# Channel mix: where the values, the sigmoid and the norm's mean stand in a round; and the last round of the time mix

## The chip, the cores and the metric

One core of a Trainium2 chip runs the whole program in one launch. The time is the device time in microseconds (us) of that core. Each of its engines has a queue of its own that it works through in order: TensorE (PE: matrix products, weight loads beside them), VectorE (DVE), ScalarE (ACT), GpSimd (POOL) and SyncE (SP), which here only issues DMAs. Engines wait for each other through semaphores.

## The reference, cut to what matters

Four layers follow each other on S = 4096 tokens of D = 256 channels: an attention with two memories, a mixture of experts, a time mix with channel mix, and a ternary feed-forward layer. The change lies in the third:

```python
# time mix, its last steps (y, new_state from the WKV recurrence)
r = sigmoid(r * tmr + x_prev * (1.0 - tmr))
x = x + r * y
# channel mix
xp = concatenate([x[:, -1:], x[:, :-1]], axis=1)
xn = _layernorm(x, g2, b2)
kk = (xn @ W_cm) * cmk4 + xp4 * (1.0 - cmk4)          # 1024 keys
rr = sigmoid(xn * cmr + xp * (1.0 - cmr))
vv = square(relu(kk)) @ W_cp
x = x + rr * vv
```

The block of tokens 0 needs the last token of the sequence as its previous one, so it is computed last.

## The kernel before, in words

Tokens are handled in NB = 8 blocks of BT = 512, channels on the partitions (256 channels = KT = 2 planes of 128; 1024 keys = KH = 8 planes, worked in PAIRS = 4 pairs). Each product of fp32 numbers is three products of high and low halves (L1468 to L1470), so every operand is split: ScalarE writes the rounded high half, VectorE subtracts it for the low half. The order on each engine is written out by hand, engine by engine, inside a program block; a new block starts when all engines have left the one before.

**The time mix block** (L1849 to L2338). In round `b` VectorE runs the recurrence (`sums`, `differences`, `exponents`, `values`, `result`), ScalarE the exponentials and, in `shares`, the sigmoid (L2170, another table than exponential and logarithm, so a table load). `result(b)` ends with xa (L2015), which GpSimd adds by DMA to `after_time_mix` in memory (L1897); when that add has landed (`xa_out`), GpSimd adds the block of `after_time_mix` to `residual_sum` (L1900). In the last round the norm of the channel mix's first block (tokens 1) is worked in between: mean, centred, squares, variance, `first_scaled` (L2035), `first_normed` (L2185, writes XN and its high half XN0h), `first_low_part` (L2039, the low half XN0l), `first_key_part`, and TensorE's `first_keys` (L2315: 16 of the first 24 products of keys, those that need only XN0h). `second_centred` (L2031) takes the mean off the second block.

**The channel mix block** (L2369 to L2770), rounds `b` = 0 to 7, with `place(b)` the block of tokens.
- TensorE, in round `b`, for each pair `i`: `up(b, i)` (12 products of keys), `down(b-1, i)` (12 products of values of the round before, into banks 6 and 7), and in between `mean(b+1)` behind `up(b, 0)` and `variance(b+1)` behind `down(b-1, 1)`. `up(b, 0)` waits for the low half of the normed input; `down(b-1, 0)` waits until the values before are taken from banks 6 and 7 (`ev_d`). In round 0, `up(0, 0)` and `up(0, 1)` are only the eight products with XN0l (L2712).
- VectorE: `keys` (L2527, reads a bank), `square_keys` (L2533), `low` (L2537, low half of the squares), `receptance` (L2517), `centre` (L2503), `scale` (L2507), `low_x` (L2511), `values` (L2544, reads banks 6 and 7), `residual` (L2551).
- ScalarE: `high` (L2643, high half of the squares), `squares` of the centred input (L2618), `deviation` (table load L2622, Ln L2624, Exp L2626), `parts` (L2611, L2613), `normed` (L2633, L2637), `sigmoid` of the receptance (table load and L2647), and `low_halves` (L2656: a check of the next layer's weights, twice a round).
- GpSimd: `sum_mean` (L2482) and `sum_squares` (L2487) add the two planes of the input and of its squares, so that one product with a matrix of 1/256 gives mean and variance.
- SP, in order: `load(b+3)` (the input and its shift by one token; waits until the place has been read by `normed` and `parts`), `store(b)` (waits for `residual(b)`), `load_sum(b+2)` (waits for the store), then a weight of the next layer in rounds 0 and 1, and a block of 1 MB of hidden weights (L2442).

Of the kernel before, what the change touches and what calls it, by code (L numbers as in the profile page):

```python
# [19 lines left out]
KT = D // 128  # L20
# [56 lines left out]
def build(nc, A):  # L77
# [5 lines left out]
    with ctx:  # L83
# [1806 lines left out]
        def _(pool):  # L1890
# [3 lines left out]
            def add_to_sum(b):  # L1894
# [4 lines left out]
                pool.wait_ge(xa_out, 16 * (b + 1))  # L1899
                pool.dma_start(byk(sx_d)[:, :, b * BT:(b + 1) * BT], byk(xa_d)[:, :, b * BT:(b + 1) * BT],  # L1900
                               accum_op=ALU.add).then_inc(sx_out, 16)
# [9 lines left out]
        def _(dve):  # L1911
# [91 lines left out]
            def result(b):  # L2003
# [4 lines left out]
                go(V.tensor_tensor(YA, prev(AV), V_, ALU.subtract))  # L2008
                dve.wait_ge(sg_d, b + 1)
# [62 lines left out]
            first_low_part()  # L2072
# [3 lines left out]
        def _(act):  # L2076
# [122 lines left out]

            A_.activation(wtm[0][:, :, :], wst, ACT.Copy).then_inc(wth_rdy, 1)  # L2200
# [17 lines left out]
            for b in range(NB):  # L2218
# [15 lines left out]
                weights(b)  # L2234
                if b + 1 < NB:
                    taken(b + 1, 1)
                    exps(b + 1)
# [3 lines left out]
                if b + 1 < NB:  # L2241
                    gates(b + 1)
                else:
                    first_normed()
                    first_key_part()
                if b + 2 < NB:
                    inner(b + 2)

        @block.tensor
        def _(pe):  # L2250
# [64 lines left out]
            def first_keys():  # L2315
# [48 lines left out]
        hm, hv = rs, in_x_tok(1536, BT)  # L2364
# [36 lines left out]
        def _(sp):  # L2401
# [43 lines left out]
            sp.wait_ge(hw_add, 16 * 16)  # L2445
            for j in range(3):
# [28 lines left out]
        def _(pool):  # L2475
            P = nc.gpsimd

            def sum_mean(b):
                pool.wait_ge(cin_ld[b % 2], loaded(b))
                pool.wait_ge(xs_rdy, b)  # L2480
# [8 lines left out]
            for b in range(1, NB + 2):  # L2489
                if b >= 2:  # L2490
                    sum_mean(b)
# [3 lines left out]
        def _(dve):  # L2495
# [57 lines left out]
            for b in range(NB):  # L2553
                nxt = b + 1 < NB
                if b >= 2:
                    values(b - 2)
# [8 lines left out]
                if b == 0:  # L2565
                    receptance(0)
                else:
                    centre(b + 1)
                for i in range(1, PAIRS):
                    keys(b, i)  # L2570
                    if b >= 1 and i == PAIRS - 1 and nxt:
# [4 lines left out]
                    if b == 0 and i == PAIRS - 2:  # L2576
                        low_x(1)
                    low(b, i - 1)
                    if b == 0 and i == 1:
                        scale(1)  # L2580
                if nxt:
                    receptance(b + 1)
            values(NB - 2)
# [854 lines left out]
```

## Time and profile before

| what | us |
|---|---|
| median of 3 runs (2006.26 to 2007.89) | 2007.76 |
| the profiled execution | 2017.27 |
| its span, first to last instruction | 2015.1 |
| channel mix: first keys to the first gates of the next layer | 1202.42 to 1419.40 |

Over the span PE is busy 91%, DVE 74%, ACT 55%, POOL 15%; the mean granted clock of TensorE is 0.955. A row of the timeline reads: start, duration, engine, line, operation, what is written from what, count; and in brackets how long the engine had been idle before, and what ended it.

### The profile page before, as it was taken

What the parts mean: (1) busy time and instruction counts of PE and PEld (TensorE: products, weight loads), DVE (VectorE), ACT (ScalarE), POOL (GpSimd) and SP (SyncE); (2) the same over time, 40 slices, a digit from 0 to 9 for tenths busy, and PEclk for the clock granted to TensorE, in tenths of its full rate; (3) what the DMA queues carried; (4) which work ended last, traced back from release to release, by engine and by line L of the source; (5) the groups of instructions that cost most, each with busy time, mean ns of one, the idle gap of its engine ahead of it and who ended that gap; (6) DMA issues with size and microseconds to landing.
All of it is one profiled execution on the core that took longest, in us unless ns stands there. A gap on an engine that the chain in (4) does not pass through costs nothing. (4 is left out here: it accounts for less than half of the span.)

```text
span 2015.1 us, 31198 instructions
## 1 busy us (share of the span) xinstructions
PE 1829.8 (91%) x10840; PEld 1563.2 (78%) x10840; DVE 1489.5 (74%) x2966; ACT 1114.9 (55%) x1987; POOL 307.6 (15%) x282
## 2 busy tenths in 40 slices
PE   8999999996499999999677758999999999999999
PEld 5688888885499999999455536677788888888887
DVE  7567888886477666766599889998676776776675
ACT  4656666653344443443688857665456456456454
POOL 0001012233333323333100011111000000000000
PEclk9999999996699999999788889999999999999999
DMA  3199434413346545344434553333333143143141
GB/s 110 50 382 404 137 119 142 145 65 107 120 97 135 114 89 115 63 74 69 126 105 91 108 106 136 148 124 123 124 138 146 36 175 145 42 176 117 53 177 64
DMA packets 107986, 251.79 MB, mean 125 GB/s; under 512 B 8992, under 2 KB 51616, under 8 KB 99616
## 3 DMA queue, kind: packets, MB, share of 16 engines
q1 hardware_dynamic: 82288, 201.16, 28.3%
q0 software_dynamic: 23680, 46.28, 12.6%
q10 hardware_dynamic: 1888, 2.67, 0.4%
q8 instruction: 75, 1.23, 0.3%
q14 instruction: 55, 0.45, 0.1%
HBM read 172.88 MB, written 107.61 MB: 139 GB/s over the span
## 5 line engine op out<-in xcount | busy, mean ns | idle before, releaser
L1542 POOL DMA_INDIRECT tokens_behind_spare_rows<-yg,row_of_token x70 | 119.2, 1702 | 298.7 <-DVE row_of_token L1733 277.0
L1666 ACT ACTIVATE h<-bank,b1s 128x256 f32<-128x256 f32 x280 | 123.7, 472 | 36.3 <-PE bank L1470 21.1
L3175 ACT ACTIVATE hidden_quarter<-hidden_quarter,scl 128x512 f32<-128x512 f32 x96 | 67.6, 721 | 118.9 <-DVE hidden_quarter L3011 118.9
L1655 ACT ACTIVATE yg<-yt,own_gates 128x256 f32<-128x256 f32 x68 | 30.9, 502 | 184.0 <-DVE yt L1728 177.2
L1223 PE MATMUL bank<-st,L 128*128 128x128 f32 x768 | 117.2, 279 | 13.3 <-DVE st L573 13.2
L957 ACT ACTIVATE L<-bank 128x512 f32<-128x512 f32 x128 | 74.5, 594 | 95.7 <-PE bank L1215 84.7
L2384 PE MATMUL bank<-split_0h,hidden_weights 128*128 128x512 f32 x320 | 126.5, 395 | 0.0
L2384 PE MATMUL bank<-split_1h,hidden_weights 128*128 128x512 f32 x320 | 125.4, 392 | 0.1
L2385 PE MATMUL bank<-split_0l,hidden_weights 128*128 128x512 f32 x320 | 125.3, 391 | 0.0
L2385 PE MATMUL bank<-split_1l,hidden_weights 128*128 128x512 f32 x320 | 125.3, 391 | 0.0
L1215 PE MATMUL bank<-L 128*128 128x128 f32 x640 | 119.1, 276 | 1.2 <-ACT L L957 1.2
L573 DVE TENSOR_TENSOR st<-st,bank 128x256 f32<-128x256 f32 x192 | 75.3, 417 | 54.0 <-PE bank L1223 53.0
L1223 PEld LDWEIGHTS bank<-st,L 128*128 128x128 f32 x768 | 100.5, 193 | 17.8 <-DVE st L573 7.0
L1214 PE MATMUL bank<-L 128*128 128x128 f32 x512 | 100.9, 279 | 0.7
L2384 PE MATMUL bank<-split_2h,hidden_weights 128*128 128x512 f32 x256 | 101.4, 396 | 0.0
L1762 DVE TENSOR_TENSOR hsl<-h,hsh 128x512 fp32r<-128x512 f32 x140 | 96.9, 692 | 4.8
L2385 PE MATMUL bank<-split_2l,hidden_weights 128*128 128x512 f32 x256 | 100.2, 391 | 0.0
L1215 PEld LDWEIGHTS bank<-L 128*128 128x128 f32 x640 | 95.1, 193 | 1.4 <-ACT L L957 1.4
L2963 DVE SCALAR_TENSOR_TENSOR hidden_quarter<-bank,scl,x_tok 128x512 f32<-128x512 f32 x64 | 47.5, 749 | 56.2 <-ACT x_tok L3138 56.2
L1468 PE MATMUL bank<-xTh,w_1h 128*128 128x256 f32 x288 | 81.7, 284 | 7.2 <-ACT h L1666 7.2
L1468 PE MATMUL bank<-xTh,w_0h 128*128 128x256 f32 x272 | 77.7, 286 | 9.8 <-DVE xTl L1720 5.2
L2970 DVE TENSOR_TENSOR split_2l<-hidden_quarter,split_2h 128x1024 fp32r<-128x1024 f32 x48 | 59.2, 1254 | 35.4 <-ACT split_2h L3157 35.4
(485 smaller groups left out, 6028.1 us busy)
## 6 DMA issues: line engine op xcount, KB each, us to landing
hidden_weights<-hidden_weight_blocks SPq DMA_DIRECT2D x64, 1024.0 KB, 4.8
z_by_expert<-zero SPq DMA_DIRECT2D x64, 520.0 KB, 15.7
hidden_weight_blocks<-in_ffn_dram SPq DMA_DIRECT2D x14, 1024.0 KB
ckb<-in_ffn_dram POOLq DMA_DIRECT2D x32, 352.0 KB, 5.0
xg<-z_by_expert SPq DMA_DIRECT2D x36, 260.0 KB
x_tok<-in_w_dram SPq DMA_DIRECT2D x8, 1024.0 KB
x_tok<-x_T SPq DMA_DIRECT2D x16, 512.0 KB, 6.1
x_tok<-after_time_mix SPq DMA_DIRECT2D x15, 512.0 KB, 8.4
```

Source lines behind the costliest of these rows:

```text
L573: V.tensor_tensor(z_ if SQUARES <= n < LEVELS - 1 else x_, x_, B[2 + j][:, 0:256], ALU.subtract if n == 0 else ALU.add).then_inc(ap_rdy, 1)
L957: A_.activation(L[:, p, j, (n + 1) % 2, :, :], src, ACT.Copy).then_inc(sq_cp, 1)
L1214: T.matmul(B[j][:, 256 * m:256 * m + 128], b_, a, start=True, stop=True)
L1215: last = T.matmul(B[j][:, 256 * m + 128:256 * m + 256], a, b_, start=True, stop=True)
L1223: last = T.matmul(B[2 + j][:, 0:256].rearrange("p (a m d) -> p a m d", a=2, m=2)[:, :, m, :], Ln[:, 2 * m + 1, :], right, start=True, stop ...
L1468: nc.tensor.matmul(out, a[0], b[0], start=first, stop=False)
L1542: pool.indirect_dma_start(x2_d, bass.IndirectOffsetOnAxis(to_row[:, j:j + 1].bitcast(u32), 0), yg[:, j, :], None, compute_op=ALU.add).then ...
L1666: nc.scalar.activation(h32[:, m, :], B[m % 4][:, 0:TT], ACT.Gelu_apprx_tanh, bias=b1s[:, e * KH + m:e * KH + m + 1]).then_inc(h_act, 1)
L1762: V.tensor_tensor(hs[1][:, m:m + 2, :], h32[:, m:m + 2, :], f32(hs[0][:, m:m + 2, :]), ALU.subtract).then_inc(h_rdy, 1)
L2384: nc.tensor.matmul(out, w, x[0], start=first, stop=False, **more)
L2385: return nc.tensor.matmul(out, w, x[1], start=False, stop=last, **more)
L3175: A_.activation(QB[to][:, m, :], src, ACT.Gelu, scale=scl[:, off[lay.name] + row:off[lay.name] + row + 1]).then_inc(g_act, 1)
```

## The change

In the time mix block: GpSimd leaves out the last round's add to `residual_sum` and its wait; VectorE takes `first_low_part` inside the last `result`, ahead of its wait for the shares; ScalarE takes `first_normed` ahead of the last `shares`, and then also loads the table of logarithms and squares the second block; TensorE takes the eight products with XN0l.

In the channel mix block: each engine's list is in another order. VectorE takes `values(b-1)` at the end of round `b`, behind the last squared keys, instead of at the start of round `b+1`; `receptance(b)` in round `b` instead of at the end of round `b-1`; `centre` ahead of the first square; `residual` behind `receptance`. ScalarE takes `sigmoid(b)` behind `squares(b+1)`. TensorE takes `mean(b+2)` at the end of round `b`. GpSimd's mean sum has a buffer of its own (`mean_halves`, before it shared `rs` with the deviation) and doesn't wait for `scale`. GpSimd issues the last add to `residual_sum` here; SP waits for the last add to `after_time_mix` ahead of the first hidden blocks.

```diff
@@ GpSimd, time mix @@
+                if b + 1 < NB:
                     pool.wait_ge(xa_out, 16 * (b + 1))
                     pool.dma_start(byk(sx_d)[...], byk(xa_d)[...], accum_op=ALU.add).then_inc(sx_out, 16)
@@ VectorE, time mix, result(b) @@
                 go(V.tensor_tensor(YA, prev(AV), V_, ALU.subtract))
+                if b == NB - 1:
+                    first_low_part()
                 dve.wait_ge(sg_d, b + 1)
@@ ScalarE, time mix @@
+            def second_squares():
+                act.wait_ge(xc_rdy, 2)
+                A_.activation(sq, IN[:, 1, 0, :, :], ACT.Square).then_inc(sqr_rdy, 1)
                 weights(b)
+                if b == NB - 1:
+                    first_normed()
...
-                    first_normed()
                     first_key_part()
+                    nc.scalar.preload_act_table_set(LOG_EXP)
+                    second_squares()
@@ TensorE, time mix, first_keys() @@
+                pe.wait_ge(xn_rdy, 1)
+                for m in range(4):
+                    for k in range(KT):
+                        last = T.matmul(B[2 + m][:, :], wcm[0][:, k, m * 128:(m + 1) * 128], XN0[1][:, k, :], start=False, stop=k == KT - 1)
+                    last.then_inc(cm_ps, 1)
@@ SP, channel mix @@
             sp.wait_ge(hw_add, 16 * 16)
+            sp.wait_ge(xa_out, 16 * NB)
@@ GpSimd, channel mix @@
                 pool.wait_ge(cin_ld[b % 2], loaded(b))
-                pool.wait_ge(xs_rdy, b)
                 pool.wait_ge(mean_ps, b)
...
-            for b in range(1, NB + 2):
-                if b >= 2:
-                    sum_mean(b)
+            sum_squares(1)
+            pool.wait_ge(xa_out, 16 * NB)
+            pool.dma_start(byk(sx_d)[:, :, S - BT:S], byk(xa_d)[:, :, S - BT:S], accum_op=ALU.add).then_inc(sx_out, 16)
+            for b in range(2, NB + 2):
+                sum_mean(b)
                 sum_squares(b)
@@ VectorE, channel mix @@
-                if b >= 2:
-                    values(b - 2)
                 if b >= 1:
                     low(b - 1, PAIRS - 1)
                 keys(b, 0)
+                if b >= 1:
+                    centre(b + 1)
                 square_keys(b, 0)
+                receptance(b)
+                if b == 0:
+                    scale(1)
                 if b >= 2:
                     residual(b - 2)
...
                     square_keys(b, i)
+                    if b >= 1 and i == PAIRS - 1:
+                        values(b - 1)
                     low(b, i - 1)
...
-                if nxt:
-                    receptance(b + 1)
@@ ScalarE, channel mix @@
             parts(0)
-            squares(1)
+            deviation(1)
             high(0, 0)
-            deviation(1)
+            normed(1)
             parts(1)
             high(0, 1)
-            normed(1)
             high(0, 2)
             sigmoid(0)
             high(0, 3)
-            sigmoid(1)
...
                 squares(b + 1)
+                sigmoid(b)
                 low_halves(b, 0)
...
-                if nxt:
-                    sigmoid(b + 1)
@@ TensorE, channel mix @@
             def mean(b):
                 pe.wait_ge(hm_rdy, b - 1)
+                pe.wait_ge(xc_rdy, b)
...
-                    if i == 0 and 1 <= b < NB:
-                        mean(b + 1)
                     if b >= 1:
                         down(b - 1, i)
-                    if i == 1 and b < NB:
+                    if i == 3 and b < NB:
+                        mean(b + 2)
+                    if i == (1 if b else 0) and b < NB:
                         variance(b + 1)
```

## Rows read from the trace of the kernel before

**Rows 1.** Busy time by round: stretch; length, then engines' busy us (instructions), granted clock, DMA share, GB/s
```profile
1202.42:1224.09 21.67, 16.11 (x53) 11.64 (x53) 21.06 (x23) 15.86 (x20) 2.54 (x2) 0.80 0.90 313
1224.09:1248.33 24.24, 23.23 (x99) 18.06 (x98) 22.84 (x25) 19.50 (x26) 3.45 (x2) 1.00 0.00 1
1248.33:1274.77 26.44, 24.28 (x102) 18.55 (x101) 24.22 (x25) 17.23 (x21) 3.57 (x2) 1.00 0.42 160
1274.77:1301.18 26.41, 24.26 (x102) 18.54 (x101) 24.19 (x25) 17.23 (x21) 2.60 (x2) 1.00 0.41 159
1301.18:1326.51 25.33, 24.27 (x102) 18.53 (x101) 23.11 (x25) 17.23 (x21) 2.58 (x2) 1.00 0.34 125
1377.18:1402.40 25.22, 23.50 (x100) 18.25 (x99) 23.92 (x25) 11.95 (x14) 3.44 (x2) 1.00 0.17 63
```
**Rows 2.** Timeline of the time mix's end and the next block's start
```profile
1185.23 1.28 ACT L2170 ACT_TABLE_LOAD   x1
1186.52 1.33 ACT L2170 ACTIVATE wkv_tmp<-wkv_tmp,uw 128x512 f32<-128x512 f32 x2
...
1189.30 1.06 ACT L2192 ACTIVATE XN0h<-XN 128x1024 fp32r<-128x1024 f32 x1
...
1190.50 0.77 PE L2323 MATMUL bank<-XN0h,wcmh 128*128 128x512 f32 x1 [14.72 <-ACT XN0h L2192]
...
1193.99 1.22 DVE L2041 TENSOR_TENSOR XN0l<-XN,XN0h 128x1024 fp32r<-128x1024 f32 x1
...
1194.59 1.22 POOL L1897 DMA_DIRECT2D after_time_mix<-wkv_tmp  x1 [9.88 <-DVE wkv_tmp L2015]
...
1195.12 1.21 DVE L2033 TENSOR_TENSOR x_tok<-x_tok,bank 128x1024 f32<-128x1024 f32 x1
...
1195.65 0.40 PE L2323 MATMUL bank<-XN0h,wcml 128*128 128x512 f32 x1
1200.90 1.15 POOL L1900 DMA_DIRECT2D residual_sum<-after_time_mix  x1 [5.09 <-POOLq L2338]
...
1201.10 1.33 ACT L2613 ACTIVATE rr<-x_tok,vec 128x512 f32<-128x512 f32 x2 [9.51 <-PEq L2338]
...
1202.42 1.53 DVE L2527 SCALAR_TENSOR_TENSOR kq<-bank,vec,kx 128x512 f32<-128x512 f32 x2 [6.09 <-PE bank L2712]
```
**Rows 3.** VectorE's timeline in round 4, whose first keys start at 1301.18
```profile
1303.76 1.22 DVE L2551 TENSOR_TENSOR x_tok<-rr,x_tok 128x1024 f32<-128x1024 f32 x1
...
1307.47 2.19 DVE L2533 SCALAR_TENSOR_TENSOR kq<-kq 128x1024 f32<-128x1024 f32 x1
...
1313.45 1.23 DVE L2507 TENSOR_TENSOR x_tok<-x_tok 128x1024 f32<-128x1024 f32 x1 [0.17 <-ACT x_tok L2626]
...
1319.45 1.23 DVE L2511 TENSOR_TENSOR XN1l<-XN,XN1h 128x1024 fp32r<-128x1024 f32 x1 [0.72 <-ACT XN1h L2637]
...
1322.86 1.41 DVE L2517 SCALAR_TENSOR_TENSOR rr<-XN,vec,rr 128x512 f32<-128x512 f32 x2
```
**Rows 4.** ScalarE's timeline in round 4
```profile
1306.14 1.06 ACT L2618 ACTIVATE x_tok<-x_tok 128x1024 f32<-128x1024 f32 x1 [1.21 <-DVE x_tok L2503]
1307.11 1.04 ACT L2656 ACTIVATE low_halves<-hidden_weights 128x1024 bf16<-128x1024 uint16 x1
...
1309.69 1.06 ACT L2643 ACTIVATE khh<-kq 128x1024 fp32r<-128x1024 f32 x1 [1.45 <-DVE kq L2533]
...
1324.30 1.06 ACT L2647 ACTIVATE rr<-rr 128x1024 f32<-128x1024 f32 x1
```
**Rows 5.** SP's store and load in round 2, and GpSimd's sum
```profile
1252.16 0.36 SPq L2430 DMA_DIRECT2D x_T<-x_tok  x1
...
1256.93 0.55 SPq L2418 DMA_DIRECT2D x_tok<-after_time_mix  x1
...
1266.69 2.28 POOL L2482 TENSOR_TENSOR x_tok<-x_tok 128x512 f32<-128x512 f32 x1 [10.96 <-DMA x_tok<-after_time_mix]
```
**Rows 6.** TensorE's timeline at the turn to round 5
```profile
1325.61 0.47 PE L1468 MATMUL bank<-khh,wcph 128*128 128x512 f32 x1 [0.99 <-DVE rr L2544]
```

More of the change, by code:

```diff
@@ L1898, in add_to_sum @@
                 pool.wait_ge(x2_out[b % 2], 16 * (b // 2 + 1))
-                pool.wait_ge(xa_out, 16 * (b + 1))
-                pool.dma_start(byk(sx_d)[:, :, b * BT:(b + 1) * BT], byk(xa_d)[:, :, b * BT:(b + 1) * BT],
-                               accum_op=ALU.add).then_inc(sx_out, 16)
+                if b + 1 < NB:
+                    pool.wait_ge(xa_out, 16 * (b + 1))
+                    pool.dma_start(byk(sx_d)[:, :, b * BT:(b + 1) * BT], byk(xa_d)[:, :, b * BT:(b + 1) * BT],
+                                   accum_op=ALU.add).then_inc(sx_out, 16)
             for done in second_sems:
@@ L2071, in _ @@
                 result(b)
-            first_low_part()
             second_centred()
@@ L2363, in build @@
         low_out = sb("low_halves", [128, 1024], mybir.dt.bfloat16, to=pd)
-        hm, hv = rs, in_x_tok(1536, BT)
+        hm, hv = sb("mean_halves", [128, BT], to=pd), in_x_tok(1536, BT)
         hm_rdy, hv_rdy = sem("mean_halves_summed"), sem("square_halves_summed")
@@ L2553, in _ @@
             for b in range(NB):
-                nxt = b + 1 < NB
-                if b >= 2:
-                    values(b - 2)
                 if b >= 1:
@@ L2561, in _ @@
                 keys(b, 0)
+                if b >= 1:
+                    centre(b + 1)
                 square_keys(b, 0)
+                receptance(b)
+                if b == 0:
+                    scale(1)
                 if b >= 2:
                     residual(b - 2)
[L2565 to L2568, printed above, removed]
                 for i in range(1, PAIRS):
                     keys(b, i)
-                    if b >= 1 and i == PAIRS - 1 and nxt:
+                    if b == 0 and i == 2:
+                        low_x(1)
+                    if b >= 1 and i == PAIRS - 1 and b + 1 < NB:
                         low_x(b + 1)
@@ L2575, in _ @@
                     square_keys(b, i)
-                    if b == 0 and i == PAIRS - 2:
-                        low_x(1)
+                    if b >= 1 and i == PAIRS - 1:
+                        values(b - 1)
                     low(b, i - 1)
-                    if b == 0 and i == 1:
-                        scale(1)
-                if nxt:
-                    receptance(b + 1)
-            values(NB - 2)
             low(NB - 1, PAIRS - 1)
@@ L2620, in deviation @@
             def deviation(b):
-                if b <= NB:
+                if 1 < b <= NB:
                     nc.scalar.preload_act_table_set(LOG_EXP)
@@ L2709, in up @@
                 if b == 0 and i < 2:
-                    for m in (2 * i, 2 * i + 1):
-                        for k in range(KT):
-                            last = nc.tensor.matmul(B[2 + m][:, :], wcm[0][:, k, m * 128:(m + 1) * 128], XN0[1][:, k, :],
-                                                    start=False, stop=k == KT - 1)
-                        last.then_inc(cm_ps, 1)
                     return
@@ L2737, in _ @@
                         up(b, i)
-                    if i == 0 and 1 <= b < NB:
-                        mean(b + 1)
                     if b >= 1:
                         down(b - 1, i)
-                    if i == 1 and b < NB:
+                    if i == 3 and b < NB:
+                        mean(b + 2)
+                    if i == (1 if b else 0) and b < NB:
                         variance(b + 1)
-                    if i == 3 and b == NB - 1:
-                        mean(NB + 1)
                     if i == 1 and b == NB:
```

## The prediction

> **What bounds the kernel now.** I read the page first: TensorE is busy 91% of the span, and the chain that ended last is almost only the last layer's products (L2384, L2385). That chain begins at 1419.4 us, when the channel mix block has ended, and it is dense from there. So whatever the channel mix ends earlier goes through to the end one for one, and the time mix tail is worth what it lets the channel mix start earlier. Next I cut the channel mix into its rounds at each first key instruction [rows 1]. Round 0 takes 21.67 us, the rounds behind it 24.24 to 26.44. In round 4 VectorE is busy 23.11 of 25.33 us, TensorE 24.27 (this counts overlapped ends; started every 0.23 us, 96 products take 21.9 and the two means 2.1, together 24.0) and ScalarE 17.2. No engine is full: a chain through all of them sets the round. The timeline of round 4 shows it [rows 3, 4]. Squared keys 1 end at 1309.66, their high half starts on ScalarE at 1309.69, then come table load, Ln and Exp, and `scale` at 1313.45: 3.76 us behind. `low_x` follows 6.00 us after `scale` (square, high half, norm, its high half). From `low_x` to the next round's first key VectorE has 7.06 us of dense work (1319.45 to 1326.51). Keys that wait for TensorE lie ahead of `scale` and cost nothing. TensorE itself stops about 1 us a round for the values' instruction (L2544) [rows 6]; that is slack, not the bound.
>
> The seam between the blocks is the other place [rows 2]. VectorE is through at 1196.33, but nobody starts before 1201.1: GpSimd must first see its last add to `after_time_mix` land (issued 1194.59, seen 1200.90, so 6.3 us) before it may issue L1900 and leave. Then VectorE waits until 1202.42 for the low products (L2712).
>
> **The seam, part by part.** ScalarE: `first_normed` (1187.76 to 1190.36, about 2.6 us) goes ahead of the table load at 1185.23. Its input is scaled by 1184.3, so it ends near 1187.8. The shares (1.28 for the table and 1.33) end 2.6 us later than before, near 1190.4. VectorE has, since L2008 at 1189.07, moved `first_low_part` (1.22) to exactly there: it runs 1190.2 to 1191.4 and covers the later shares. The same five instructions follow L2008 as before in another order, so `second_centred` still starts at 1195.12 and ends 1196.33; the last xa is 1.13 later, and with it the add: issued 1195.7, landed near 1202.0. TensorE's 16 products start at 1187.8 instead of 1190.50; they took 5.5 us to 1196.0, the eight low ones 3.5 in the next block, so all end by 1196.8 at the latest. ScalarE now also squares block 1: 1196.35 to 1197.4. GpSimd no longer waits for the add to land. So the last to leave is ScalarE at 1197.4 and the next block starts at 1197.6: 3.5 us earlier. If GpSimd's issue (1195.7 plus 1.22) must end first, nothing changes.
>
> In the new block the keys' products are there already, so the first key starts at 1197.6, not at 1202.42: 4.8 us. What was behind the removed wait: GpSimd now does the squares' half sum, then waits until 1202 for the add and issues its DMA, and its first mean sum needs the load that SP issued before, which is not in by then. SP gets one more wait (1202) ahead of the three hidden blocks. Behind it is `load(3)`, which waits for `parts(1)` near 1208 anyway, and ScalarE wants the first hidden block only at 1215. Bounds for this wait: 0, and 3 us if the blocks land late; I take 0.
>
> **Round 0.** VectorE's list: 4 keys (1.44 each), 4 squares (1.14), 4 low halves (1.13), receptance 1.32, scale 1.14, low_x 1.14: 18.5 us. Receptance 1 (1.32) has gone to round 1 and the waits with it. ScalarE stays ahead of each: Exp ends near 1201.5 and `scale` comes at 1201.6; normed and its high half are ready at 1205.5 for a `low_x` at 1207.9. One collision may stay. When GpSimd adds while VectorE works from SBUF alone, VectorE's instruction takes 1.0 us more (2.19 against 1.23 in the row at 1307.47 [rows 3]); keys read PSUM and are not held up (1316.95 to 1318.2 in round 4). I take half of it, 0.6. Round 1 starts at 1216.7 instead of 1224.09: **-7.4 us**, 1.3 of which are only handed on.
>
> `mean(2)` now stands in TensorE's queue ahead of `up(1,0)`. Its load is issued by 1201.3 and lands between 5 and 9.8 us later [rows 5], its sum and mean take 2.3: 1208.6 to 1213.4. `up(1,0)` needs 2.7 us, or 5.1 at the 1.2 GHz level, which the rows show behind idle stretches (products every 0.43 us instead of 0.23). So it is there at 1211.3 to 1218.5, around 1216.7. I take 0; the bad end is +1.8.
>
> **A later round.** Offsets from the first key. VectorE: key 0, centre 1.37, square 2.51, receptance 3.65, residual 4.97, key 6.10, square 7.54. ScalarE: high half 3.77, squares 4.74 (4.96 before), and then what is new here: table load and sigmoid (1.28 and 1.06), 5.82 to 8.1, then the low halves (1.04 and 0.19), so high half 1 starts at 9.28. Before it was 1309.69 - 1301.18 = 8.51 [rows 1, 4]: **+0.77**. It was bound by the square, itself held 1.05 by GpSimd; that sum now falls at 6.2 to 7.4, under the PSUM keys, but this no longer helps, as ScalarE is late. From there 3.76 and 6.00 us as before, since all their members stay. Behind `low_x`: square, values, low, low; receptance is gone, **-1.32**. The moved `values` wait for the last down product (offset 19.4; they come at 21.3), and TensorE needs them only behind `up(b+1,0)` at 23.1, so its 1 us stop goes, for nothing. Sum: 25.33 + 0.77 - 1.32 = 24.8 us.
>
> The price of the moved load is its row: 1.28 us at 1185.23, and the next instruction 0.01 us behind it at 1186.52 [rows 2]. The Trainium skill ("ScalarE: Activation LUTs", section "What ACT_TABLE_LOAD costs") adds a drain of about 1380 ns to each load's 1283 ns; this trace doesn't show the drain, and by it the round would be an estimated 26.2 us.
>
> **The mean a round ahead.** In PE's queue it was behind `up(b,0)` of its own round; now it is ahead of `up(b+1,0)`, 2.7 us sooner, while its data come later: the load follows the store of residual(b-2), whose end moves from offset 3.8 to 6.2. From store to GpSimd's sum took 14.5 us in round 2 (1252.16 to 1266.69 [rows 5]); by the same timeline 14.4, 11.9, 13.1 and 10.4 in rounds 3 to 6. So the sum starts at 20.8, 20.6, 18.2, 19.4, 16.7. In round 2 it runs 21.4 to 22.6, the mean to 23.65, both first products to 26.5, and the second half of the next key, due at 25.5, ends 1.1 late. Behind such a delay TensorE runs late through the next round and holds `scale` by 0.35. Round 4 loses 0.3 and round 5 loses 1.1 to the sum's collision with `low_x` or a square. Rounds 2 to 6: 25.9, 26.25, 25.45, 25.9, 24.8 = 128.3, against 26.44 + 26.41 + 25.33 + 25.34 + 25.33 = 128.85: **-0.55**. Bounds: 124.0 if nothing of this bites, 133 if each is late by one more us.
>
> Round 1 goes from 24.24 to 24.8: **+0.55**. Round 7 gets receptance 7 but loses the collision (its mean sum falls at 16.5 to 17.7, under keys): `centre(9)` at 22.96 against 22.95. From there squares, half sum and variance lead to the same end: **0**; +0.8 if the collision stays.
>
> **Sum.** -7.4 + 0.55 - 0.55 + 0 = -7.4 us. The profiled execution took 2017.27 us (span 2015.1 and 2.2 around it) and would take 2009.9; it lies 9.5 above the median of 2007.76, so the forecast is **2000.4 us**. Its own range is 1998 to 2003.
>
> **Rivals.** B, rounds tighter (0.14): no late load, no collision, rounds 2 to 6 in 124.0. For it: 24.0 is TensorE's floor and VectorE needs 21.9. Against: the slow loads of rounds 2 and 3. Time 2000.4 - 4.3 = 1996.1.
> C, later means (0.16): hidden blocks and loads collide once more and the means cost 1 us in each of five rounds: 2005.4. For it: 14.5 us in round 2. Against: rounds 4 to 6 have room.
> D, round 0 gives half back (0.08): `up(1,0)` or the hidden blocks late by 3 to 4 us: 2004.
> E, slower (0.07): the mean in front of `up(b+1,0)` closes a loop: residual 6.2, load 14.5, sum 1.2, mean 1.05, first product 1.4, back at the key after 24.4 us, 0.4 short of the round. If the load takes 3 us more in each round 1 to 6 than in round 2, some 2 us a round are lost beyond C's five: -7.4 + 5 + 12 = +9.6, 2017. It decides from about 16.5 us between store and sum; no row has that.
> F, a stop behind the moved table load (0.03): if ScalarE lost the load's own length once more, 1.28 us, in each of seven rounds, 2000.4 + 9.0 = 2009.4. Against it: the 0.01 us behind the load in every row. It is the drain of the Trainium skill's "ScalarE: Activation LUTs", put in this kernel's terms.
> G, my own case: 0.52.
>
> 0.2% of the time, 4.0 us, is what a measurement can tell from no change. Faster: G, B and the better third of C, 0.72. Same: the rest of C and D, 0.18. Slower: E and F, 0.10. The range 1995.5 to 2005.8 leaves out E, F and the far end of B, with chance about 0.15 to 0.2.
>
> **What would show it.** The first key at 1197.6, the second round's at 1216.7. In later rounds: high half 1 about 9.3 behind the first key (if 8.5, the sigmoid is not the bound), no wait of down products for L2544, TensorE waiting for GpSimd's half sum (about 1 us ahead of the variance), and in rounds 2 and 3 a wait of the mean for its sum. The forecast falls if the rounds differ from 24.8 to 26.3, or if the block starts no earlier than 1200.

## The result and the profile after

The change makes the kernel a little faster: 2002.97 us median of 8 runs (1997.58 to 2004.02) against 2008.49 of 8 runs of the kernel before (2006.26 to 2011.68), ratio 0.9967 [0.9956, 0.9978], so 6.6 us by the ratio and 5.5 by the medians. The forecast was 2000.4, or 7.4 us less, with a range of 1998 to 2003: the median lies at the upper edge of it.

The profiled executions took 2017.27 and 2002.26 us, and that is not the gain. At the last instruction of VectorE ahead of the moved low part (1189.07 before, 1180.86 after) the second is already 8.21 us ahead, in stages that the change doesn't touch; the profiled execution of the kernel before was a long one, 8.8 above the median of its runs. At the first gate instruction of the next layer it is 6.77 further ahead. These 6.77 us are the gain as the traces show it, and 8.21 + 6.77 = 14.98 is the whole distance. So from here on times are counted from that instruction, called the anchor. Starts of the rounds' first keys, of the next layer, and the steps between them:

```
              r0     r1     r2     r3     r4     r5     r6     r7     next
before start  13.35  35.02  59.26  85.70 112.11 137.44 162.78 188.11 231.13
       length 21.67  24.24  26.44  26.41  25.33  25.34  25.33  43.02
forecast      19.1   24.8   25.9   26.25  25.45  25.9   24.8   43.0
after  start   8.80  29.49  53.18  78.09 105.64 131.11 156.28 180.86 224.36
       length 20.69  23.69  24.91  27.55  25.47  25.17  24.58  43.50
```

Busy time by round after, with the columns of [rows 1]. Rounds 0 to 3 and 6, then round 7 up to `centre(9)`:

```profile
1189.66:1210.35 20.69, 16.57 (x48) 11.82 (x49) 19.65 (x20) 15.02 (x20) 4.21 (x3) 0.75 1.05 344
1210.35:1234.04 23.69, 23.07 (x98) 18.11 (x97) 22.52 (x25) 16.83 (x22) 3.53 (x2) 1.00 0.03 10
1234.04:1258.95 24.91, 21.89 (x93) 16.80 (x92) 22.04 (x25) 17.00 (x21) 2.77 (x2) 1.00 0.45 170
1258.95:1286.50 27.55, 25.48 (x102) 19.59 (x101) 22.13 (x25) 17.03 (x21) 3.62 (x2) 0.94 0.40 153
...
1337.14:1361.72 24.58, 23.99 (x101) 18.60 (x100) 22.03 (x25) 17.01 (x21) 2.78 (x2) 1.00 0.29 108
1361.72:1385.17 23.45, 21.68 (x91) 16.66 (x90) 21.92 (x24) 13.05 (x15) 3.50 (x2) 1.00 0.20 68
```

Three things differ from the forecast: round 0 is 1.6 us longer, round 1 is 1.1 shorter, and of rounds 2 to 6 (127.68 together against 128.3) round 3 is 1.3 longer, round 2 is 1.0 and round 5 is 0.7 shorter.

The seam after, which answers to [rows 2] (start, length, engine, line, operation, idle before and what ended it). GpSimd's last add to `after_time_mix`, its half sum, the add to `residual_sum` and the mean's sum; ScalarE's new squares; VectorE's low part, last centred block, first key and `scale`; TensorE's variance:

```profile
1187.53 1.20 POOL L1897 DMA_DIRECT2D after_time_mix<-wkv_tmp  x1 [11.08 <-DVE wkv_tmp L2018]
1189.65 1.26 POOL L2501 TENSOR_TENSOR x_tok<-x_tok 128x512 f32<-128x512 f32 x1 [0.93 <-POOLq L2352]
1193.86 1.16 POOL L2505 DMA_DIRECT2D residual_sum<-after_time_mix  x1 [2.94 <-DMA after_time_mix<-wkv_tmp]
1201.36 1.79 POOL L2496 TENSOR_TENSOR mean_halves<-x_tok 128x512 f32<-128x512 f32 x1 [6.34 <-DMA x_tok<-after_time_mix]
...
1188.16 1.06 ACT L2204 ACTIVATE x_tok<-x_tok 128x1024 f32<-128x1024 f32 x1 [3.49 <-DVE x_tok L2036]
...
1182.12 1.23 DVE L2044 TENSOR_TENSOR XN0l<-XN,XN0h 128x1024 fp32r<-128x1024 f32 x1
...
1186.92 1.21 DVE L2036 TENSOR_TENSOR x_tok<-x_tok,bank 128x1024 f32<-128x1024 f32 x1
1189.66 1.41 DVE L2543 SCALAR_TENSOR_TENSOR kq<-bank,vec,kx 128x512 f32<-128x512 f32 x2 [1.53 <-PEq L2352]
...
1194.52 1.23 DVE L2523 TENSOR_TENSOR x_tok<-x_tok 128x1024 f32<-128x1024 f32 x1 [0.87 <-ACT x_tok L2637]
...
1201.95 2.28 DVE L2549 SCALAR_TENSOR_TENSOR kq<-kq 128x1024 f32<-128x1024 f32 x1
...
1191.06 2.05 PE L2713 MATMUL bank<-x_tok,avg 128*128 128x512 f32 x2 [3.96 <-POOL x_tok L2501]
```

GpSimd starts its half sum at 1189.65 in the new block and sees the add land only at 1193.8: the 5.09 us that it stood still ahead of the block's end [rows 2] are gone. ScalarE's squares (to 1189.22) are the last to end, and the first key follows at 1189.66, 8.80 behind the anchor.

In the steady state (round 6), ScalarE up to its high half 1, and VectorE's `scale` and `low_x`; these answer to [rows 3, 4]:

```profile
1342.86 1.28 ACT L2658 ACT_TABLE_LOAD   x1
1344.16 1.06 ACT L2658 ACTIVATE rr<-rr 128x1024 f32<-128x1024 f32 x1
...
1346.16 1.05 ACT L2654 ACTIVATE khh<-kq 128x1024 fp32r<-128x1024 f32 x1
...
1349.90 1.23 DVE L2523 TENSOR_TENSOR x_tok<-x_tok 128x1024 f32<-128x1024 f32 x1 [0.78 <-ACT x_tok L2637]
...
1355.90 1.30 DVE L2527 TENSOR_TENSOR XN1l<-XN,XN1h 128x1024 fp32r<-128x1024 f32 x1 [1.05 <-ACT XN1h L2648]
```

High half 1 starts 9.02 behind the first key (1337.14), `scale` 3.74 behind that, `low_x` 6.00 behind `scale`, the next key 5.82 behind `low_x`: 24.58. Each part is within 0.3 us of the one forecast (9.28, 3.76, 6.00, 5.74).

### The profile page after: what moved, and what is told of

Its sections match the earlier page's. It is cut to its first block and busy times, and to the rows that moved or that the text cites. A ratio compares the mean times of both kernels' runs of the same rounds, so it can differ in the third digit from the quotient of the medians.

```text
span 2000.2 us, 31208 instructions
## 1 busy us (share of the span) xinstructions
PE 1826.2 (91%) x10840; PEld 1561.7 (78%) x10840; DVE 1479.8 (74%) x2966; ACT 1113.1 (56%) x1987; POOL 308.5 (15%) x282
## 3 DMA queue, kind: packets, MB, share of 16 engines
q8 instruction: 75, 1.23, 0.3%
## 5 line engine op out<-in xcount | busy, mean ns | idle before, releaser
L1666 ACT ACTIVATE h<-bank,b1s 128x256 f32<-128x256 f32 x280 | 123.6, 471 | 35.0 <-PE bank L1470 20.3
L1215 PEld LDWEIGHTS bank<-L 128*128 128x128 f32 x640 | 95.5, 194 | 0.0
L1214 PEld LDWEIGHTS bank<-L 128*128 128x128 f32 x512 | 79.3, 194 | 7.2 <-issue 2.7
```

The source lines that it names most:

```text
L1214: T.matmul(B[j][:, 256 * m:256 * m + 128], b_, a, start=True, stop=True)
L1215: last = T.matmul(B[j][:, 256 * m + 128:256 * m + 256], a, b_, start=True, stop=True)
L1666: nc.scalar.activation(h32[:, m, :], B[m % 4][:, 0:TT], ACT.Gelu_apprx_tanh, bias=b1s[:, e * KH + m:e * KH + m + 1]).then_inc(h_act, 1)
```

## Experiments

Two theories stood for the gain: the seam (time mix tail, GpSimd's wait) makes it and the new order of the rounds adds next to nothing; or both give part. And two for what the rounds lose: the place of `mean` in TensorE's queue together with data that come late, or the table load ahead of ScalarE's high half 1. All kernels are the changed one with the edit shown, but for the fifth. The kernel before was run again beside them: 2009.18 us (18 runs) beside e1 to e4, 2010.17 (15 runs) beside e5 to e8; the ratios, with their 95% intervals, are to these. A summary ahead of the single ones: the lengths of the rounds, and under `next` the start of the next layer counted from each kernel's own anchor (231.13 before):

```
kernel             median   ratio  95%               r0    r1    r2    r3    r4    r5    r6    r7    next
changed            2002.97  0.9967 [0.9956, 0.9978]  20.69 23.69 24.91 27.55 25.47 25.17 24.58 43.5  224.36
e1_seam_wait       2007.42  0.9995 [0.9986, 1.0004]  20.94 26.25 25.02 27.50 25.50 25.10 24.50 43.5  231.46
e2_mean_behind     1996.64  0.9945 [0.9928, 0.9961]  19.79 24.98 25.07 24.50 24.61 24.94 24.51 43.5  220.73
e3_sigmoid_last    2003.29  0.9965 [0.9952, 0.9979]  19.62 25.77 26.47 25.92 25.49 24.95 24.77 43.2  225.03
e4_both            1998.66  0.9949 [0.9936, 0.9963]  20.72 25.01 25.03 24.24 25.34 25.04 24.24 43.3  221.67
e5_seam_alone      2003.71  0.9962 [0.9952, 0.9972]  20.09 24.20 26.43 26.36 25.32 25.34 25.33 43.1  224.94
e6_residual_first  1994.92  0.9914 [0.9897, 0.9931]  18.69 25.34 23.72 24.82 23.70 23.75 23.71 43.3  215.80
e7_load_first      1997.67  0.9939 [0.9927, 0.9952]  20.90 25.79 24.51 24.50 24.51 24.52 24.51 43.5  221.55
e8_all             1995.22  0.9920 [0.9907, 0.9933]  18.68 25.34 23.71 23.71 23.71 23.72 24.82 43.3  215.78
```

### e1_seam_wait: GpSimd's last add waits in the time mix again

```diff
-                if b + 1 < NB:
-                    pool.wait_ge(xa_out, 16 * (b + 1))
-                    pool.dma_start(... accum_op=ALU.add).then_inc(sx_out, 16)
+                pool.wait_ge(xa_out, 16 * (b + 1))
+                pool.dma_start(... accum_op=ALU.add).then_inc(sx_out, 16)
...
-            pool.wait_ge(xa_out, 16 * NB)
-            pool.dma_start(...sx_d[:, :, S - BT:S] ... accum_op=ALU.add).then_inc(sx_out, 16)
```

> The changed kernel, only that GpSimd again waits in the time mix block for its last add to after_time_mix to land, and issues the last add to residual_sum there. Theory 1 (the seam): that wait alone kept the other engines; the next block starts 3.3 us later than in the changed kernel, all rounds behind it stay, and the time is 3.3 us above the changed kernel's (ratio to before about 0.998). Theory 2 (absorbed): round 0 took 20.7 us in the changed kernel where 18.5 of work stood, so its own waits (loads, variance) end last and swallow the shift: under 1 us above the changed kernel.

Ratio 0.9995 [0.9986, 1.0004]: nothing is left of the gain. The first key comes at 13.15, so this one wait is worth 4.35 us, not the 3.3 expected: the last add is issued 6.67 us behind the anchor here and 5.52 before, since `first_low_part` now stands ahead of the last xa, and the wait moves with it. GpSimd's rows around it, with the wait at the block's end back:

```profile
1185.29 1.22 POOL L1897 DMA_DIRECT2D after_time_mix<-wkv_tmp  x1 [11.21 <-DVE wkv_tmp L2017]
1191.48 1.15 POOL L1900 DMA_DIRECT2D residual_sum<-after_time_mix  x1 [4.98 <-POOLq L2351]
```

Another 2.56 us went in round 1 (26.25 against 23.69). TensorE there, its variance and the products behind it, and two windows with the granted clock (third number from the end):

```profile
1219.82 2.07 PE L2710 MATMUL bank<-x_tok,avg 128*128 128x512 f32 x2 [3.13 <-POOL x_tok L2500]
...
1222.12 0.63 PE L1469 MATMUL bank<-XN1l,wcmh 128*128 128x512 f32 x1
...
1215.00:1220.00 5.00, 1.87 (x9) 1.25 (x8) 4.97 (x7) 3.59 (x4) 1.51 (x2) 0.90 0.00 0
1220.00:1225.00 5.00, 5.00 (x10) 3.29 (x11) 3.50 (x3) 4.46 (x7) 1.98 (x1) 0.50 0.01 3
```

The variance starts 7.11 behind the round's first key, just as in the changed kernel (1217.48, 7.13 behind), because GpSimd's half sum sets it in both. But here TensorE had run out of work 3.13 us before, not 0.62, and behind that idle stretch it was granted half its clock, the 1.2 GHz level, in the whole second window. The longer stop has two reasons. TensorE took its mean 8.3 us ahead of the key here and 7.1 there; and there it went through the round's first products at a granted clock of 0.77 (1205 to 1210), here at the full clock (1.00). So it was through 4.0 us behind the key here and 6.5 there. The 2.56 us came by way of the clock. The traces of the other kernels differ in rounds 0 and 1 as well, as the section on the forecast shows; whether each run of e1 loses these 2.56 us is not shown, but its median lost more than 4.35.

### e2_mean_behind: the mean behind the first products of its round

```diff
+                    if i == 0 and 1 <= b < NB:
+                        mean(b + 1)
                     if b >= 1:
                         down(b - 1, i)
-                    if i == 3 and b < NB:
+                    if i == 3 and b == NB - 1:
                         mean(b + 2)
```

> The changed kernel, only that mean(b+1) stands behind up(b,0) again in TensorE's queue, as before, instead of at the end of the round before. Theory 1 (late mean): TensorE no longer waits for GpSimd's sum ahead of up(b+1,0); rounds 2 and 3 go from 24.9 and 27.6 to about 24.6 each, round 4 from 25.5 to 24.6, in all 3 to 4 us below the changed kernel (ratio to before about 0.995). Theory 2 (slack): VectorE and ScalarE set the round anyway and the wait only moved: within 0.7 us of the changed kernel, and round 3 stays above 26.

1996.64 us, 0.9945 [0.9928, 0.9961]. The changed kernel at the turn of rounds 3 and 4, GpSimd's mean sum, TensorE's mean, VectorE's first key, and the clock of the 6 us:

```profile
1280.06 2.13 POOL L2496 TENSOR_TENSOR mean_halves<-x_tok 128x512 f32<-128x512 f32 x1 [13.17 <-DMA x_tok<-after_time_mix]
...
1282.24 1.96 PE L2709 MATMUL bank<-mean_halves,avg 128*128 128x512 f32 x2 [2.07 <-POOL mean_halves L2496]
...
1286.50 0.75 DVE L2543 SCALAR_TENSOR_TENSOR kq<-bank,vec,kx 128x512 f32<-128x512 f32 x1 [1.98 <-PE bank L1470]
...
1280.00:1286.00 6.00, 3.93 (x9) 2.31 (x9) 4.52 (x5) 1.06 (x1) 2.13 (x1) 0.72 0.00 0
```

The load's data come 14.3 us behind the store that it follows (1265.77), TensorE waits 2.07 for the sum, falls to half clock behind the wait, and the key is 1.98 late. (0.8 us of the sum's 2.13 is a collision with VectorE's square.) With the mean behind `up(b,0)` the same data are as late (the sum at 1251.57 in round 2, 15.5 us behind the store at 1236.10), but nobody waits for them; the mean follows `up(b,0)` directly:

```profile
1251.57 1.30 POOL L2496 TENSOR_TENSOR mean_halves<-x_tok 128x512 f32<-128x512 f32 x1 [14.35 <-DMA x_tok<-after_time_mix]
...
1252.92 1.12 PE L2709 MATMUL bank<-mean_halves,avg 128*128 128x512 f32 x2
```

Rounds 2 to 6 sum to 123.6 instead of 127.7, though round 2 stays at 25.07, and the next layer starts 3.6 us earlier. Moving the mean forward was the part of the change that cost time. (The intervals of the two ratios overlap a little; the traces and e7 carry the reading.)

### e3_sigmoid_last: sigmoid and its table load behind the last high half

```diff
                 squares(b + 1)
-                sigmoid(b)
+                if b == NB - 1:
+                    sigmoid(b)
...
                 high(b, 3)
+                if nxt:
+                    sigmoid(b)
```

> The changed kernel, only that sigmoid(b) with its table load stands behind high(b,3) on ScalarE in rounds 1 to 6, not ahead of the first low halves. Theory 1 (ScalarE is last): high half 1 comes 8.4 to 8.8 us behind the round's first key instead of 9.0 to 9.3, set by the square, and each undisturbed round falls from 24.6 to about 24.2; 2 us in all. Theory 2 (another bound): high half 1 moves but scale or low_x waits for something else, and the rounds stay at 24.6 (within 0.5 us in all).

2003.29 us, 0.9965 [0.9952, 0.9979]: no difference from the changed kernel. ScalarE's high half 1 in round 6 (first key at 1338.14) now waits for VectorE's square:

```profile
1346.88 1.06 ACT L2654 ACTIVATE khh<-kq 128x1024 fp32r<-128x1024 f32 x1 [1.99 <-DVE kq L2549]
```

That is 8.74 behind the key instead of 9.02: ScalarE has 1.99 us to spare, and the round gains 0.28 at best. The sigmoid holds the round by no more than that. Nor did the 24.2 us and the 2 us in all of the first theory come: in round 6 `low_x` took 1.75 us beside GpSimd's sum instead of 1.23, and the round 24.77. The late means are still there (rounds 2 and 3 take 26.47 and 25.92); TensorE's slow stretch falls in round 2 this time, behind a wait of 2.81.

### e4_both: e2 and e3 together

> Both edits: mean behind up(b,0), and sigmoid behind high(b,3). If the two costs are separate they add: 5 to 6 us below the changed kernel, rounds 2 to 6 all near 24.2. If TensorE's own work (24.0 us a round) becomes the bound, the sum is smaller: 4 us, and TensorE's waits in a round add to less than 0.3 us.

The edit is both diffs above. 1998.66 us, 0.9949 [0.9936, 0.9963]. Its clean rounds take 24.24 us (3 and 6), 0.26 less than in e2, but not all five are clean as expected: they sum to 123.9, e2's to 123.6. The sums of GpSimd now fall on other instructions, as at the end of round 2, where VectorE's last two low halves take 3.14 instead of 2.35 beside the sum that GpSimd starts at 1256.09:

```profile
1256.46 3.14 DVE L2553 TENSOR_TENSOR khl<-kq,khh 128x1024 fp32r<-128x1024 f32 x2
```

The other 0.95 us by which its trace ends behind e2's stand in rounds 0 and 1.

### e5_seam_alone: the kernel before with the seam's edits only

The time mix tail, the second block's squares and low products, GpSimd's moved DMA and SP's wait are the changed kernel's; the rounds of all engines are in the old order. Against the changed kernel, for VectorE (ScalarE and TensorE likewise):

```diff
+                if b >= 2:
+                    values(b - 2)
...
-                receptance(b)
...
-                    if b >= 1 and i == PAIRS - 1:
-                        values(b - 1)
                     low(b, i - 1)
...
+                if nxt:
+                    receptance(b + 1)
+            values(NB - 2)
```

> The kernel before with only the seam's part of the change: normed input, its low products and second squares in the time mix block, the last add to residual_sum moved into the channel mix, no wait for it at the end of the block; round 1 to 7 keep the order of before. Theory 1 (the seam is the whole gain): first keys 4.5 us earlier, rounds 1 to 7 as before (24.2, 26.4, 26.4, then 25.3), 4 to 6 us below before (ratio about 0.9975). Theory 2 (the parts need each other): round 0 in the old order waits for the variance or for the sigmoid and gives the 4.5 us back: within 2 us of before.

2003.71 us, 0.9962 [0.9952, 0.9972]. The first key comes at 8.81, and rounds 1 to 6 are those of the kernel before to 0.05 us. Round 0 is 1.6 us shorter too (20.09 for 21.67), with the second block's squares and the low products done before it begins. It ends 6.19 us earlier than before; the whole change ends 6.77 earlier. With e1 this settles where the gain is: the seam without the new rounds has it, the new rounds without the seam have nothing that the runs can tell from zero.

### e6_residual_first: e4, and residual and second square ahead of receptance

The edit beyond e4's:

```diff
                 square_keys(b, 0)
-                receptance(b)
+                if b == 0 or b == NB - 1:
+                    receptance(b)
...
                     square_keys(b, i)
+                    if 1 <= b < NB - 1 and i == 1:
+                        receptance(b)
```

> Mean behind up(b,0) and sigmoid behind high(b,3) as in the run with both edits, and in rounds 1 to 6 VectorE takes receptance(b) behind the second squared keys instead of behind the first, so the residual and the second squares come 1.3 us earlier. Theory 1 (the chain square 1, high half 1, table, Ln, Exp, scale, low_x sets the round): high half 1 starts 7.45 us behind the first key instead of 8.74, VectorE's idle time ahead of scale goes, and the rounds fall from 24.2 to 25.0 to 24.0, TensorE's own work; 2 to 4 us below the run with both edits. Theory 2 (TensorE or the half sums already set it): the rounds stay, within 0.7 us in all.

1994.92 us, 0.9914 [0.9897, 0.9931], the lowest median; e8's interval is about the same. In e3 the square of keys 1 set the round. Taking receptance (1.33) out from ahead of it lets the high half start 8.20 behind the key instead of 8.74 (not at 7.45 as expected: the square now takes 2.01 us beside GpSimd's half sum), and rounds 2 and 3 become:

```profile
1234.89:1258.61 23.72, 23.72 (x102) 18.70 (x101) 22.65 (x25) 17.14 (x22) 3.47 (x2) 1.00 0.47 178
1258.61:1283.43 24.82, 24.82 (x106) 19.59 (x105) 23.75 (x25) 17.15 (x22) 2.65 (x2) 1.00 0.45 170
```

The first, 0.52 shorter than e4's clean rounds, is busy on TensorE throughout; the 24.0 expected was 0.3 too much. The second carries a collision of GpSimd's sum with a square:

```profile
1277.61 1.35 POOL L2496 TENSOR_TENSOR mean_halves<-x_tok 128x512 f32<-128x512 f32 x1 [11.91 <-DMA x_tok<-after_time_mix]
...
1277.73 2.32 DVE L2549 SCALAR_TENSOR_TENSOR kq<-kq 128x1024 f32<-128x1024 f32 x1
```

### e7_load_first: SP issues the token load ahead of the bulk transfers

```diff
+                if 1 <= b:
+                    bulk_loads(b - 1)
                 store(b)
...
-                if b < 2:
-                    weights(names[b][0])
-                if b + 3 < NB:
-                    sp.wait_ge(lows_rdy, 2 * b + 2)
-                    hidden_block(b % 3, summed[b + 3])
```

`bulk_loads` holds the removed lines; so the bulk transfers (1 MB of hidden weights, and in rounds 2 and 3 a weight of the next layer) stand behind the load, not between store and load. The mean keeps the place that the change gave it.

> The changed kernel, mean still a round ahead, only that SP issues each 1 MB of hidden weights (and of the next layer's weights, rounds 0 and 1) behind the next load of a token block instead of ahead of it. Theory 1 (the data are late): from store to GpSimd's mean sum 11 us or less instead of 14.3 to 14.8 in rounds 2 and 3, TensorE doesn't wait for the sum, rounds 2 and 3 take 24.9 or less and 24.6, in all about 3 us below the changed kernel. Theory 2 (the place in TensorE's queue costs by itself, whatever the data): rounds 2 and 3 stay at 24.9 and 27.6.

1997.67 us, 0.9939 [0.9927, 0.9952]. SP's issues in round 2 in the changed kernel, then here with GpSimd's sum:

```profile
1240.19 0.36 SPq L2444 DMA_DIRECT2D x_T<-x_tok  x1
...
1243.87 0.46 SPq L2456 DMA_DIRECT2D hidden_weights<-hidden_weight_blocks  x1
...
1245.28 0.36 SPq L2432 DMA_DIRECT2D x_tok<-after_time_mix  x1
...
1255.00 1.28 POOL L2496 TENSOR_TENSOR mean_halves<-x_tok 128x512 f32<-128x512 f32 x1 [13.69 <-DMA x_tok<-after_time_mix]
```

```profile
1238.53 0.36 SPq L2444 DMA_DIRECT2D x_T<-x_tok  x1
...
1242.20 0.47 SPq L2432 DMA_DIRECT2D x_tok<-after_time_mix  x1
...
1243.54 0.33 SPq L2456 DMA_DIRECT2D hidden_weights<-hidden_weight_blocks  x1
...
1247.77 2.04 POOL L2500 TENSOR_TENSOR mean_halves<-x_tok 128x512 f32<-128x512 f32 x1 [8.11 <-DMA x_tok<-after_time_mix]
```

From the store to the sum it is 14.8 us in the one and 9.2 in the other (in round 3 it is 14.3 and 11.1). The second of the two load instructions is issued 3.7 us behind the store instead of 5.1; so 1.4 of the 5.6 us is the place in SP's queue, and the other 4.2 lie behind the issue, where the load no longer has the bulk transfers ahead of it. Rounds 2 to 6 take 24.50 to 24.52, in step. So e2 and e7 cure the same loss from its two ends: rounds 2 to 6 sum to 4.1 and 5.1 us less than in the changed kernel. The traces end 3.6 and 2.8 earlier; e7's lost 2.3 in rounds 0 and 1, where its mean waited 6.29 us and ran at half clock.

### e8_all: e6 and e7 together

> Mean behind up(b,0), sigmoid behind high(b,3), receptance behind the second squares, and the loads of token blocks ahead of the 1 MB weights. With the mean behind up(b,0) its sum is early enough, so the order of the loads should add nothing to the run without it, or 0.5 us if it moves GpSimd's sums off VectorE's instructions; 10 to 13 us below before (ratio 0.994 or less).

The edit is the diffs of e6 and e7. 1995.22 us, 0.9920 [0.9907, 0.9933], the same as e6, as expected, and more below before than the 10 to 13 us of the expectation. Its rounds 2 to 5 are all at one length, with TensorE busy in all of it:

```profile
1257.77:1281.48 23.71, 23.71 (x102) 18.66 (x101) 22.64 (x26) 17.14 (x22) 3.05 (x2) 1.00 0.47 178
```

This is the floor of the round with these products; the forecast put TensorE's own work at 24.0. VectorE is busy 22.64 of it and ScalarE 17.14, so a shorter round would need fewer products. The collision of e6's round 3 is gone there, but another one sits in round 6 (24.82), so the two end 0.02 us apart.

## Why the forecast was right, and which terms were off

**The seam: right.** The block's first instruction, SP's load, starts 8.68 behind the anchor instead of 12.01, 3.33 earlier (forecast 3.5), and the first key 4.55 earlier (4.8). The order of events is the one forecast: ScalarE's squares are last to end, not GpSimd's issue. SP's new wait lasted 1.1 us and nothing behind it was late; I had taken 0 of 0 to 3.

**Rounds 0 and 1: nearly right together, each off by itself.** Forecast was 19.1 + 24.8 = 43.9 us, measured 20.69 + 23.69 = 44.38, so only 5.5 us were handed on to round 1 where 7.4 were forecast, and round 1 gave 1.1 back. "Exp ends near 1201.5 and `scale` comes at 1201.6" is the sentence that failed. I had laid out ScalarE's chain with full-speed products in it. The variance in front of Ln took 2.05 us, at the 1.2 GHz level behind 3.96 idle us, and `scale` waited 0.87 for it. The other part is the collision, of which I had taken half: the square at 1201.95 took 2.28, and all 1.06 us of it counted. Neither is a fixed price. The same stretch in e6, whose edits change nothing in round 0 but that the mean no longer stands at its end (the windows of rounds 0 and 1, TensorE's variance, then GpSimd's mean sum and VectorE's keys beside it):

```profile
1190.86:1209.55 18.69, 13.67 (x53) 9.69 (x54) 18.52 (x21) 15.03 (x20) 3.72 (x3) 1.00 1.03 331
1209.55:1234.89 25.34, 23.47 (x93) 17.95 (x92) 22.84 (x24) 18.04 (x23) 3.26 (x2) 0.93 0.12 46
...
1192.26 1.10 PE L2719 MATMUL bank<-x_tok,avg 128*128 128x512 f32 x2 [2.86 <-POOL x_tok L2501]
...
1204.41 1.30 POOL L2496 TENSOR_TENSOR mean_halves<-x_tok 128x512 f32<-128x512 f32 x1 [8.70 <-DMA x_tok<-after_time_mix]
...
1204.61 1.41 DVE L2543 SCALAR_TENSOR_TENSOR kq<-bank,vec,kx 128x512 f32<-128x512 f32 x2
```

Here the low products had ended 1.1 us nearer to the variance and the clock held, and GpSimd's sum came later and fell on keys, which it doesn't hold up. Round 0 took 18.69, close to the 18.5 of work that the forecast had added up. Of the nine kernels with the new seam or part of it, five show this (idle 2.82 to 2.88, variance 1.10) and four the slow form (idle 3.79 to 9.08, variance 2.05). The fork lies ahead of the anchor, where no edit reaches. In the four, the time mix took 24.3 to 24.7 us from the anchor's instruction of round 5 to that of round 6, in the five 23.5 (as in the kernel before). And of its 24 products of first keys the first 8 or 9 stood over 0.4 us apart in the four, at half clock, in the five the first 14. Where the full clock came sooner, TensorE was done sooner, stopped longer ahead of the variance and fell back. How the longer round of the time mix goes with this is not shown. Rounds 0 and 1 together take 44.0 to 47.2 us over them, 44.3 in e5, and the forecast of 43.9 is at the fast end. The runs of the changed kernel, 1997.6 to 2004.0, are spread over 6.4 us, so these 3.2 may be one part of that spread; I have the clock of that stretch only for the profiled ones.

Round 1 is a miss of its own. I had given it the steady 24.8, but its lists are shorter: VectorE has no `residual` yet (1.22), and round 0 computes a sigmoid at its own end and the table stays, so no load (1.28) stands ahead of round 1's. ScalarE there, its sigmoid and its high half 1:

```profile
1215.97 1.04 ACT L2658 ACTIVATE rr<-rr 128x1024 f32<-128x1024 f32 x1
...
1218.54 1.06 ACT L2654 ACTIVATE khh<-kq 128x1024 fp32r<-128x1024 f32 x1 [0.50 <-DVE kq L2549]
```

High half 1 starts 8.19 behind the first key (1210.35), not 9.28, and that is the whole 1.1 us; the parts behind it are those of the steady round. So the sign was wrong: -0.55 for +0.55. That it made good part of round 0's miss is luck.

**Steady rounds: right in mechanism, and nearly in size.** 24.58 in round 6 against 24.8. The table load took 1.28 us, and the next instruction started 0.02 behind it (1342.86 to 1344.16), so the drain of rival F did not come, and the Trainium skill's 1380 ns ("ScalarE: Activation LUTs", section "What ACT_TABLE_LOAD costs") does not show in this trace either. `values` waits for no down product any more, and TensorE's stop of [rows 6] went, for nothing. What I had not seen: of the term +0.77 for the sigmoid (measured: +0.51, 9.02 for 8.51) little could be had back. Without it (e3) the square holds the high half at 8.74.

**Late means: right place, wrong sum in one round.** Round 2 was forecast at 25.9 and took 24.91: the mean waited 2.94 us, the key was only 0.33 late. Round 3 was forecast at 26.25 and took 27.55. It is 2.97 over round 6: its last part, `low_x` to the next key, has 1.98 more, and its `scale` comes 1.0 late, since TensorE was late from the turn before; for these I had 1.1 and 0.35. The wait of 2.07 was in the forecast's reach; what was missing is that TensorE ran the mean and the next products at half clock behind it, which e1 shows again in its rounds 1 and 3. Round 4's 25.47 against 25.45 is luck: its own loss of 0.3 did not come, and the handed-on one was 1.0 there too. Rounds 2 to 6 gave -1.17 against -0.55; rounds 2 and 3 nearly cancel, and rounds 5 and 6 were 0.7 and 0.2 shorter than forecast. e2 and e7 show that the cause is the mean's place and its late data: with the loads cured all five rounds are 24.5, with the mean behind the first products they are 24.5 to 25.1.

**Round 7: the collision stayed**, 43.5 against 43.0, +0.5 where +0.8 was the bad end. `scale` comes 12.76 behind the first key, before it was 12.27, and the low half beside GpSimd's mean sum takes 2.3 us in both.

**Sum.** By the table: seam and round 0 -5.53, round 1 -0.55, rounds 2 to 6 -1.17, round 7 +0.48: -6.77, against -7.4 + 0.55 - 0.55 + 0. The net is close, by 0.6 us, since what was missing from the seam and round 0 (1.9) and round 7 (0.5) came back in round 1 (1.1) and rounds 2 to 6 (0.6): part of the hit is luck. Of the rivals, C (later means) is true in part, above all in round 3. D had round 0 giving some back, which it did, but by late first products or hidden blocks, and neither was late. E did not come, as the longest way from store to sum was 14.8 us and its point was 16.5. B, rounds at TensorE's floor, took the further edits of e6.

What stays open: how much of round 3's loss is the clock and how much the late data alone. e2 and e7 take both away at once. The traces give an estimate. In the changed kernel the clock held behind round 2's stop and fell behind round 3's, in e3 it was the other way round: round 2 takes 24.91 and 26.47, round 3 27.55 and 25.92. So the clock is worth about 1.6 us each time, if e3's place of the sigmoid (0.3 at most) is left aside, and the other 1.4 us of round 3's 2.97 are the late data.

## What to carry to other kernels

An engine that waits for a transfer to land just ahead of a block's end holds all engines: look there first, and move the wait to the first use of the data behind the boundary (4.35 us here, two thirds of the 6.77 that the traces show). Before moving a reduction forward in TensorE's queue, compare the moment its data arrive with the moment that its new place comes up; ahead of the next round's products it costs its wait and perhaps the clock as well, behind them it was free. When a round is a chain through several engines, taking out one link gives only the slack up to the next: the sigmoid 0.27 us a round (24.51 to 24.24), the receptance ahead of the square then 0.53 more (to 23.71), where TensorE has no gap left.

## What the runs showed of the hardware

**Idle TensorE and its clock.** The length of a stop does not tell whether the granted clock falls to its 1.2 GHz level. Of the mean's and the variance's instructions behind a stop of 1.8 us or more in the channel mix of the nine profiled executions, those behind 3.13, 3.28, 3.32, 3.79, 3.96, 4.00, 5.97, 6.29 and 9.08 us were slow (2.05 to 2.08 for the 128x512 pair, products every 0.43). Behind shorter ones both occur: held behind 2.08, 2.82 to 2.88 (five), 2.94 and 3.01 us (1.10 to 1.12), fallen behind 2.07, 2.08 and 2.81 (1.96 to 2.08), and falling within the pair behind 1.86, 1.87 and 2.72 (1.33 to 1.44). The same stop at the end of round 3 came out slow in the changed kernel and in e1, and fast in e3. The held one of round 2 in the changed kernel:

```profile
1256.34 1.12 PE L2709 MATMUL bank<-mean_halves,avg 128*128 128x512 f32 x2 [2.94 <-POOL mean_halves L2496]
...
1257.53 0.39 PE L1469 MATMUL bank<-XN1l,wcmh 128*128 128x512 f32 x1
```

So a forecast for this kernel has to price a stop of 2 to 3 us both ways.

**VectorE and GpSimd on SBUF.** The price of a collision is what is left of the other's instruction. In e6 GpSimd's sum ends at 1277.61 + 1.35 = 1278.96, and the square that had started at 1277.73 ends at 1280.05, 1.09 later, nearly as if it began there (alone it takes 1.22). In round 0 the same: 1201.36 + 1.79 = 1203.15, and the square ends at 1204.23, 1.08 later. The other way round, the sum of 1280.06 (2.13 instead of 1.3) ends 1.13 behind the square that VectorE had begun at 1279.84 (1.22). VectorE's instructions that read a PSUM bank (L2543, L2560) are not held: e6's two keys at 1204.61 take 1.41 us under GpSimd's sum, as they do without it. The Trainium skill says this as a rule ("SBUF — State Buffer", section "SBUF: two separate sides": whichever of the two starts first holds the shared pair of ports for its whole instruction), and the rows agree. I had used a flat 1.0 us.

**One DMA's wait behind others.** In rounds 2 and 3, with 1 MB of hidden weights and a weight of the next layer issued between, GpSimd's sum of a loaded block (512 KB) started 14.15 to 15.47 us behind the store in the traces with that order, and 9.2 to 11.1 us in e7 and e8, with the bulk behind the load.
